# Two causal attention stages, the norm's root and TensorE filler products rearranged in an eight-stage kernel

## The reference

```python
x = x + jnp.tanh(g_xattn[0]) * _L0_xattn_ref(_layernorm(x), ctx_512, ...)   # causal, 16 heads, 64 keys used
x = x + jnp.tanh(g_ffn[0]) * _L0_ffn_ref(_layernorm(x), ...)                # top 8 of 64 experts' biases
x = x + jnp.tanh(g_xattn[1]) * _L1_xattn_ref(_layernorm(x), ctx_512, ...)   # latent, 1500 keys
x = x + jnp.tanh(g_ffn[1]) * _L1_ffn_ref(_layernorm(x), ...)                # ternary weights: mean |w| is needed
x = x + jnp.tanh(g_xattn[2]) * _L2_xattn_ref(_layernorm(x), ctx_512, ...)   # latent, queries with rope
x = x + jnp.tanh(g_ffn[2]) * _L2_ffn_ref(_layernorm(x), ...)                # Hadamard
x = x + jnp.tanh(g_xattn[3]) * _L3_xattn_ref(_layernorm(x), ctx_512, ...)   # causal again
x = x + jnp.tanh(g_ffn[3]) * _L3_ffn_ref(_layernorm(x), ...)                # 8 experts, one per row, and a shared one
return x

def causal(q, latent_kv):                     # layers 0 and 3, in short
    k, v = jnp.split(latent_kv @ Wkv_expand.T, 2, axis=-1)
    scores = jnp.einsum('bhqd,bhkd->bhqk', heads(q @ Wq.T), heads(k)) * inv_sqrt_d
    attn = jax.nn.softmax(jnp.where(causal, scores, min), axis=-1)
    return merge(jnp.einsum('bhqk,bhkd->bhqd', attn, heads(v))) @ Wout.T
```

## Time and profile before

| | us |
|---|---|
| median of 3 runs | 1805.56 (1804.91 to 1805.61) |
| profiled execution | 1805.35 |
| its span, first to last instruction | 1803.5 |
| busy in the span: PE, DVE, ACT, POOL | 1607.6, 922.1, 634.8, 670.5 |

### The profile page before, as it was taken

One profiled execution on the slowest core, in us unless ns is written; L12 is line 12 of the kernel. 1 busy time (PEld: TensorE's weight loads), 2 busy tenths in 40 slices (PEclk: granted clock), 3 DMA queues, 4 the chain that ended last, 5 costly groups with the idle time before them and its releaser, 6 DMA issues. The chain is left out here.

```text
span 1803.5 us, 38433 instructions
## 1 busy us (share of the span) xinstructions
PE 1607.6 (89%) x16648; PEld 1197.8 (66%) x16660; DVE 922.1 (51%) x1587; ACT 634.8 (35%) x941; POOL 670.5 (37%) x479
## 2 busy tenths in 40 slices
PE   6757889999999996668997999999999989777998
PEld 3335478888888875455443888888888745434466
DVE  2964165565665626772445565665655232147312
ACT  3323334454444431224011454544444221133221
POOL 2504255654446100640764645655441030232101
PEclk9977899999999997777998999999999989778999
DMA  7053365445554023001314555445540200512401
GB/s 122 1 164 95 85 140 131 101 110 113 118 124 93 26 79 105 0 1 67 94 23 102 131 126 117 98 106 118 113 92 16 82 0 0 194 56 63 134 24 59
DMA packets 64424, 154.39 MB, mean 86 GB/s; under 512 B 14428, under 2 KB 43676, under 8 KB 63344
## 3 DMA queue, kind: packets, MB, share of 16 engines
q1 hardware_dynamic: 63488, 150.10, 33.8%
q0 software_dynamic: 768, 1.84, 0.3%
HBM read 87.51 MB, written 5.51 MB: 52 GB/s over the span
## 5 line engine op out<-in xcount | busy, mean ns | idle before, releaser
L1390 DVE TENSOR_REDUCE latent_psW<-latent_psW 128x1 f32<-128x500 f32 x654 | 418.4, 682 | 221.7 <-PE latent_psW L1288 221.3
L1368 ACT ACTIVATE latent_w<-latent_psS 125x896 f32<-125x896 f32 x384 | 351.8, 919 | 432.8 <-PE latent_psS L1306 429.1
L1316 PEld LDWEIGHTS latent_psO<-latent_val,latent_w 125*64 125x64 f32 x10752 | 323.6, 138 | 30.6 <-issue 17.1
L1316 PE MATMUL latent_psO<-latent_val,latent_w 125*64 125x65 f32 x10752 | 340.9, 223 | 0.0
L1305 PE MATMUL latent_psS<-latent_qA,latent_kA 128*125 128x448 f32 x768 | 290.1, 378 | 3.9 <-DVE latent_qB L1406 2.3
L1306 PE MATMUL latent_psS<-latent_qB,latent_kB 128*125 128x448 f32 x768 | 282.3, 368 | 0.0
L1288 PE MATMUL latent_psW<-latent_kA,latent_qA 128*128 128x500 f32 x654 | 214.6, 398 | 12.5 <-DMA latent_qA<-latent_qh 11.2
L1305 PEld LDWEIGHTS latent_psS<-latent_qA,latent_kA 128*125 128x125 f32 x768 | 143.2, 186 | 30.9 <-ACT latent_w L1368 4.6
L1306 PEld LDWEIGHTS latent_psS<-latent_qB,latent_kB 128*125 128x125 f32 x768 | 143.5, 187 | 19.7
L1288 PEld LDWEIGHTS latent_psW<-latent_kA,latent_qA 128*128 128x128 f32 x654 | 125.3, 192 | 29.8 <-POOL latent_kB L1262 12.7
L794 POOL TENSOR_TENSOR latent_rawT<-latent_rawT,latent_ropeT 128x1000 f32<-128x1000 f32 x48 | 110.5, 2328 | 33.4 <-DMA latent_rawT<-in_ctx_cols 21.0
(11 more groups left out here) (332 smaller groups left out, 2110.7 us busy)
## 6 DMA issues: line engine op xcount, KB each, us to landing
latent_qA<-latent_qh SPq DMA_DIRECT2D x128, 112.0 KB, 2.3
latent_rawT<-in_ctx_cols SPq DMA_DIRECT2D x32, 375.0 KB, 5.2
latent_rawT<-in_ctx_cols SPq DMA_DIRECT2D x64, 187.5 KB, 5.8
latent_raw<-in_ctx SPq DMA_DIRECT2D x32, 375.0 KB
latent_kA<-latent_high SPq DMA_DIRECT2D x32, 375.0 KB, 3.7
latent_kB<-latent_high SPq DMA_DIRECT2D x32, 375.0 KB, 5.6
latent_kA<-latent_rawT SPq DMA_DIRECT2D x32, 375.0 KB, 5.2
experts_wgu<-in_L_gu SPq DMA_DIRECT2D x8, 1024.0 KB, 16.2
```

The lines of the kernel that those rows point to most:

```text
L1316: last = pe.matmul(sums[r:r + 64, c, :], w[t % ROUND][:, c * 128 + r:c * 128 + r + 64], val[b % 2][:, t, :], start=(t == 0 and c == 0), st ...
L1368: act.activation(w[t % ROUND][:, :].rearrange("p (h n) -> p h n", h=2), psS[0:KP, t % 2, :, 0:GH], ACT.Exp).then_inc(exp_done, 1)
L1390: dve.tensor_reduce(bank[:, THIRD + j:THIRD + j + 1], bank[:, 0:THIRD], mybir.AxisListType.X, ALU.max).then_inc(max_ready, 1)
```

## The change

In the causal stages the sixteen value products before the loop are gone. `expand_values(p)` makes the values of one pair in step p of the loop, behind the scores of that pair, into both halves of `ps_y`, the bank that the projection also uses; it waits until DVE has added pair p-4 and ACT has copied the values before. ACT's `take_values(p)` copies them in two pieces. The norm's root is the first thing on ACT; in stage 3 the turning also comes before the key products. In stage 0 the magnitudes come in eight DMAs and eight reductions, one behind the normalising of each pair, each of which takes the sum of the one before as its first element. The 64-row operands become 128-row ones whose lower half is cleared.

The weights of causal stage 3 are loaded in the Hadamard stage, and keep their place when the arena is made anew. In the top-8 stage all eight turns come first (two groups of four, one ACT copy each), then the eight products. In both query stages ACT makes the root before or between the fold copies. In the Hadamard stage POOL waits for DVE's small scalings. `keep_busy` puts products of the identity with itself, which nobody reads, into places where PE waits: 8 in `begin`, 14 and 36 in the top-8 stage, 18 in each latent stage, 16 in the Hadamard stage, 10 in causal stage 3, 18 in the experts stage.

```diff
+
+
+def keep_busy(pe, g, to, count):
+
+    for _ in range(count):
+        pe.matmul(to, g.ident[:, :], g.ident[:, :], start=True, stop=True)
...
+        self.root(act)
+        self.scalar_tiles(act)
+
+    def root(self, act):
         g = self.g
         if self.moments:
             act.wait_ge(self.mv_ready, NT)
         act.activation(self.std[:, :], g.mv[:, :, 1], ACT.Sqrt, bias=g.eps[0:TP, 0:1]).then_inc(self.std_ready, 1)
+
+    def scalar_tiles(self, act):
...
     w = Weights(nc, g, f"xattn{layer}_w")
-    w.wkv = w.put([DC, 2 * C], (None, d[f"L{layer}_kv"]))
-
-    w.ctxT = w.put([DC, B, 2, SK], (None, d["ctx_first"].rearrange("d (b e k) -> d b e k", b=B, e=2)))
+    w.wkv = w.put([128, 2 * C], (lambda v: v[0:DC, :], d[f"L{layer}_kv"]))
+
+    w.ctxT = w.put([128, B, 2, SK], (lambda v: v[0:DC, :, :, :], d["ctx_first"].rearrange("d (b e k) -> d b e k", b=B, e=2)))
+    w.pads = [w.wkv[DC:128, :], w.ctxT[DC:128, :, :, :]]
...
+                def turn_rows():
+                    norm.tensor(pe)
+                    pe.wait_ge(norm.xnT_ready, NT)
+
+                if layer:
+                    keep_busy(pe, g, ps_a[:, 0, 0:128], 10)
+                    turn_rows()
...
-                for b in range(B):
-                    pe.wait_ge(taken, n - 1)
-                    pe.matmul(ps_a[:, n % 2, 0:C], ctxT[:, b, :, :], wkv[:, C:2 * C],
-                              start=True, stop=True).then_inc(prod, 1)
-                    n += 1
-                norm.tensor(pe)
-                pe.wait_ge(norm.xnT_ready, NT)
+                if not layer:
+                    turn_rows()
...
+
+                def expand_values(p):
+                    wait_from(pe, x_done, p - 3)
+                    wait_from(pe, v_taken, p)
+                    for e in range(2):
+                        last = pe.matmul(ps_y[:, e * C:(e + 1) * C], ctxT[:, 2 * p + e, :, :], wkv[:, C:2 * C], start=True, stop=True)
+                    last.then_inc(v_done, 1)
...
                 def project(p):
                     pe.wait_ge(o_taken, p + 1)
+                    pe.wait_ge(v_taken, min(p + 4, NP))
                     if p >= 1:
...
                 for p in range(NP + 3):
                     if p < NP:
                         scores(p)
+                        expand_values(p)
+                    if 2 <= p < NP + 2:
+                        turn_weights(p - 2)
                     if 2 <= p < NP + 2:
                         output(p - 2)
...
             def _(act):
-                n = 0
-                for c in range(CC):
-                    for h in range(2):
+                def take_keys():
+                    for n in range(KV):
+                        c, h = n // 2, n % 2
                         act.wait_ge(prod, n + 1)
                         act.copy(kT[:, c, 8 * h:8 * h + 8, :],
                                  ps_a[:, n % 2, :].rearrange("p (b k) -> p b k", k=SK)).then_inc(taken, 1)
-                        n += 1
-                act.wait_ge(zeroed, 1)
-                for b in range(B):
+
+                norm.root(act)
+                if not layer:
+                    take_keys()
+                norm.scalar_tiles(act)
+                if layer:
+                    take_keys()
+                for n in range(KV, KV + QQ):
+                    m, h = (n - KV) // 2, n % 2
                     act.wait_ge(prod, n + 1)
-                    v = ps_a[:, n % 2, 0:C].rearrange("p (j e k) -> p j e k", j=HP, e=2)
-                    act.copy(values[0:64, b, :, 0, :], v[0:64, :, 0, :])
-                    act.copy(values[64:128, b, :, 1, :], v[64:128, :, 1, :]).then_inc(taken, 1)
-                    n += 1
-                norm.scalar(act)
-                for m in range(CC):
-                    for h in range(2):
-                        act.wait_ge(prod, n + 1)
-                        act.mul(qT[:, m, h * HALF:(h + 1) * HALF], ps_a[:, n % 2, 0:HALF], HD ** -0.5).then_inc(taken, 1)
-                        n += 1
+                    act.mul(qT[:, m, h * HALF:(h + 1) * HALF], ps_a[:, n % 2, 0:HALF], HD ** -0.5).then_inc(taken, 1)
+
+                def take_values(p):
+                    act.wait_ge(v_done, p + 1)
+                    if p == 0:
+                        act.wait_ge(zeroed, 1)
+                    v = ps_y[:, :].rearrange("p (b j e k) -> p b j e k", b=2, j=HP, e=2)
+                    for e in range(2):
+                        last = act.copy(values[64 * e:64 * e + 64, 2 * p:2 * p + 2, :, e, :], v[64 * e:64 * e + 64, :, :, e, :])
+                    last.then_inc(v_taken, 1)
 
                 def exp(p):
                     act.wait_ge(shifted, p + 1)
                     act.activation(sc[:, p % 3, :, :], sc[:, p % 3, :, :], ACT.Exp).then_inc(exp_done, 1)
 
-                def take(p):
+                def take_weights(p):
                     for h in range(2):
                         act.wait_ge(turned, 2 * p + h + 1)
                         if p >= 2 and h == 0:
                             act.wait_ge(o_done, p - 1)
                         act.copy(wT[:, p % 2, 4 * h:4 * h + 4, :],
                                  ps_t[:, h, :].rearrange("p (j n) -> p j n", j=4)).then_inc(wT_ready, 1)
+
+                def take_output(p):
                     act.wait_ge(o_done, p + 1)
                     act.copy(oT[:, :, p * TP:(p + 1) * TP].rearrange("q c (e s) -> q c e s", e=2),
                              ps_o[:, 0:256].rearrange("q (c e s) -> q c e s", c=2, e=2)[:, :, :, 0:S]).then_inc(o_taken, 1)
 
                 for p in range(NP + 2):
+                    if p < NP:
+                        take_values(p)
                     if p >= 2:
-                        take(p - 2)
+                        take_weights(p - 2)
+                        take_output(p - 2)
...
                 if magnitudes is not None:
-                    dve.wait_ge(lanes_came, 16)
-                    dve.tensor_reduce(magnitudes, lanes[:, :], X, ALU.add, apply_absolute_value=True).then_inc(lanes_summed, 1)
+                    dve.memset(lanes[:, 0, 0:1], 0.0).then_inc(lanes_summed, 1)
+
+                def sum_magnitudes(m):
+                    dve.wait_ge(lanes_came[m], 16)
+                    dve.wait_ge(lanes_summed, m + 1)
+                    dve.tensor_reduce(lanes[:, m + 1, 0:1] if m + 1 < CHUNKS else magnitudes, lanes[:, m, :], X, ALU.add,
+                                      apply_absolute_value=True).then_inc(lanes_summed, 1)
 
                 def soft(p):
                     u = p % 2
                         soft(p)
                     if 1 <= p <= NP:
                         normalise(p - 1)
+                        if magnitudes is not None:
+                            sum_magnitudes(p - 1)
 
 
 def top8_weights(nc, g, d):
     w = Weights(nc, g, "ffn0_w")
     w.rw = w.put([128, CC, 64], (None, d["L0_rw"].rearrange("(c p) n -> p c n", p=128)))
     w.bias = w.put([TP, 64], (None, d["L0_rb"].partition_broadcast(TP)))
-    w.eb = w.put([64, C], (None, d["L0_eb"]))
+    w.eb = w.put([128, C], (lambda v: v[0:64, :], d["L0_eb"]))
+    w.pads = [w.eb[64:128, :]]
     return w
 
 
...
                 ahead.clear(pool)
+                ahead.cleared_all(pool)
+                weights.pad(pool)
+                pool.memset(wT[E:128, :, :], 0.0).then_inc(wT_padded, 1)
...
                 for t in range(NT):
-                    if t >= 2:
-                        pe.wait_ge(wT_ready, t - 1)
-                    pe.transpose(ps_t[0:E, t % 2, 0:TP], e[:, t, :], g.ident[0:TP, 0:TP]).then_inc(turned, 1)
-                    pe.wait_ge(wT_ready, t + 1)
+                    pe.transpose(ps_t[0:E, t // 4, t % 4 * TP:(t % 4 + 1) * TP], e[:, t, :], g.ident[0:TP, 0:TP]).then_inc(turned, 1)
+                weights.padded_all(pe)
+                pe.wait_ge(wT_padded, 1)
+                for t in range(NT):
+                    pe.wait_ge(wT_ready, t // 4 + 1)
                     if t >= 2:
                         pe.wait_ge(y_taken, t - 1)
-                    pe.matmul(ps_y[0:TP, t % 2, 0:C], wT[:, t, :], eb[:, :], start=True, stop=True).then_inc(y_done, 1)
+                    pe.matmul(ps_y[0:TP, t % 2, 0:C], wT[:, t // 4, t % 4 * TP:(t % 4 + 1) * TP], eb[:, :], start=True, stop=True).then_inc(y_done, 1)
 
...
-                for t in range(NT):
-                    act.wait_ge(turned, t + 1)
-                    act.copy(wT[:, t, :], ps_t[0:E, t % 2, 0:TP]).then_inc(wT_ready, 1)
+                for half in range(2):
+                    act.wait_ge(turned, 4 * half + 4)
+                    act.copy(wT[0:E, half, :], ps_t[0:E, half, 0:4 * TP]).then_inc(wT_ready, 1)
...
+                    if n == 2:
+                        norm.root(act)
+                norm.scalar_tiles(act)
...
+                norm.root(act)
                 for h in range(NH):
...
+                keep_busy(pe, g, psO[:, 0:128], 18)
...
             def _(pool):
+                pool.wait_ge(had_ready, CC + 2)
...
```

(12 more changed lines are left out.)

66 lines of the change are left out of this document (49 added, 17 removed).

## The result

| | before | changed |
|---|---|---|
| median, us | 1805.39 (1804.91 to 1805.61, 4 runs) | 1749.14 (1744.18 to 1749.90, 4 runs) |
| profiled execution | 1805.35 | 1744.18 |
| its span | 1803.5 | 1742.4 |

What follows compares the result with a forecast made beforehand. The prediction saw barrier-separated stages, each bound by its own last chain, with gains where PE is slow or idle. Stage savings summed to 54.3 us, taking 1805.35 to 1751 us, range 1733 to 1771.

Steps and rivals of the forecast that it cites:

- 25.2 forecast for the front: Causal stage 3, barrier to first score product: 21.8 us instead of 47.0, so 25.2 us saved.
- 4.4 lost in the loop: Causal stage 3 loop: value products lengthen pairs from 5.76 to 6.9 us; four pairs counted, 4.4 us lost.
- rival (e): Causal stage 3: the early weight load does not do what it says; no loss, the turning covers it; no chance given.
- the clock term: Causal stage 3 front: fillers at the slow clock, then keys half fast, half slow, taken as 5.4 us.
- 9.1 forecast: Causal stage 0, net saving: 23.7 us saved at the front, 14.6 lost to magnitude pieces in the loop.
- rival (c): Causal loops: value products waiting for the residual add four pairs back close a ring; 12 + 5 us worse, 1768; chance 0.10.
- 5.8 forecast for the new order: Top-8 stage: turns grouped ahead of the products, bound by DVE's passes, save 5.8 us; its 36 fillers taken as 0.
- 10.6 and 1.9 forecast: Query stages 1 and 2: the earlier root removes waits before turning, saving 10.6 and 1.9 us.
- 4.0 forecast: Hadamard stage: POOL waits for DVE's scalings, PE starts earlier behind 16 fillers; 4.0 us saved, bounds 6 and -1.7.
- (a): Whole kernel: the clock does not come up, all fillers slow; 32 us worse, 1783, about 1767 if half; chance 0.12.
- (b): Whole kernel: the clock stays up through the turning; keys, queries, router products and folds fast; 17 us better, 1734; chance 0.15.
- (d): Causal loops: PE and DVE stop overlapping through the shared bank; 55 + 45 us worse, 1851; chance 0.03.

Runs made afterwards that it cites:

- e10: The kernel before the change, with only ACT's root moved ahead of its key and value copies in both causal stages; 1803.57 us, ratio 0.9985.
- e4: The changed kernel with the sixteen value products ahead of the causal loops again; 1756.07 us, ratio 0.9712.
- e2: The changed kernel with key, value and top-8 products over the 64 used rows again, fillers kept; 1755.69 us, ratio 0.9739.
- e1: The changed kernel with every filler product taken out; 1747.62 us, ratio 0.9682.
- second chip run: The changed kernel, unaltered, run again on another chip; median 1751.04 us, ratio 0.9679.
- e9_late_load: The changed kernel with causal stage 3's weights loaded in that stage again and POOL clearing the pads there; 1747.65 us, ratio 0.9689.

## Why the prediction was right, point by point

**The causal stage 3** was sized well: 25.2 forecast for the front, 26.0 measured; 4.4 lost in the loop, 3.2 measured (56.8 against 53.6). Its parts: the root alone 3.5 us (e10), the value products in the loop instead of ahead 7.4 us (e4), the cleared rows 4.5 us (e2), the ten fillers 0.5 us at most (e1). If the parts add, that leaves some 7 us of the 22.8 for the turning ahead of the keys, in the time in which PE waited for weights; this was not run alone. The early load is worth nothing in the total, as rival (e) had it; ahead of the turning it also keeps POOL's clearing away from DVE's scaling, which the prediction did not count.

**The cause of the clock term was wrong.** The step of the sum that failed is "the ten fillers take 2.1 us (fast) to 4.5 us (slow) ... Keys 3.6 us fast, 7.2 slow; I take 5.4", which let the fillers bring the clock up. The keys took 5.9 us with and without fillers, and 7.19 with 64-row operands. The clock comes up by the end of the keys when they are 128-row products, and it did not when they were 64-row ones; I had taken that edit for free. The fillers were not at the slow clock either, as I had them: they took 2.47 us. The Trainium skill (TensorE: Matmul & The Clock Gate, Part 4) says that turning does not count as work for the clock as other products do. By that rule fillers ahead of the turning are wasted. The two keys' rows agree with it; the router products of the top-8 stage, fast behind fillers and a turning in eight profiles of eleven and never without fillers, do not. The same page of the Trainium skill says in its closing table that a product over 32 rows takes as long as one over 128. For 64 rows the duration agrees at the same clock (1.13 us for four records in both kernels), and it can't be used for the granted clock, which differed.

**Causal stage 0.** 9.1 forecast, 7.7 and 2.7 measured. The first maximum came where it was forecast within 2.3 us, pairs at 7.65 for 7.8. The term that was too small is the loop's: 67.9 us from first maximum to last add, against 50.3 before, so 17.6 lost where I had 14.6. Of the 3 us between, 2.3 lie in the pairs of 8.5 and 9.0 us (10.96 on the second chip run): e9_late_load, which has no such pairs, has a loop of 65.6. In the pair of 8.5 us DVE's normalisation took 2.08 us instead of 1.23, beside a POOL product that began with it (54.24 and 54.29); e4_values_ahead, which has no value products in the loop, has that pair too (8.51). Behind it PE stood 4.86 us for the residual add and was then at half clock. This is rival (c) once, not in every pair; in e9_late_load the normalisation took 1.23 us, PE waited 2.43, the clock stayed up and the pairs were 7.64. The 2 us between the two profiles in the front have a like cause. In the first, DVE's scaling took 4.13 us and was over when POOL's key products began at 19.19; in the second the keys were faster (3.92 us instead of 5.53), POOL began at 17.54, beside the scaling, and that took 7.08 us; the turning was then full of waits, and the queries began 0.4 us later and at half clock (7.88 us instead of 6.28). All six profiles with keys of 3.9 us in stage 0 have a scaling of 7.1 us and queries of 7.8 to 9.1, so faster keys did not make this front shorter. In my account of stage 0 before, only 2.9 us of the reduction showed; e10 showed that with an early root it still ended at 57.0, its operands having landed at 39.8: the transfer and the reduction behind it alone made a front of that length.

**Top-8 stage.** 5.8 forecast for the new order; without fillers the stage was 5.5 us shorter than before. With fillers it was another 1.5 to 4.1 us shorter, which I had counted at 0 for the 36. Most of it is not theirs: the router products, behind the 14, took 3.27 us instead of 6.10 where the stage gained 4.1, and 6.10 as before where it gained 1.5. The sum has no term for them.

**Query stages.** 10.6 and 1.9 forecast; 12.2 to 13.0 and 4.0 to 4.1 measured, and undoing the root's place alone cost 11.9 and 4.1 us. The mechanism was the one named; in stage 2 the sum counted the wait only, and the clock behind it was missing: turning and the 32 records behind it took 4.0 and 4.46 us, where they took 4.6 and 5.91 in the kernel before.

**Hadamard stage.** 4.0 forecast, 2.7 measured. POOL's wait is worth 2.2 us, the fillers 0.4. I had PE start at 4.2 us after the barrier; the sixteen fillers ran until 5.3, at half clock for 3.4 us of it.

**Latent and experts stages.** The fillers made the first products of the latent stages faster (0.92 us for three records instead of 1.59), but DVE sets the pace there. Latent stage 2 came out 1.5 to 1.6 us longer, where I had 0.3 saved; e1_no_fillers puts that down to the fillers. Latent stage 1 shows nothing either way. In the experts stage the router products took 6.01 us as before; the 1.9 us saved are near the 1.5 forecast.

**The rivals.** (a) is out in its form, the granted clock being 0.95 and 0.85 in the top-8 stage; (b) did not happen, since in stage 3 the queries took 6.3 us but the keys 5.9, and the router products of the experts stage were as slow as before; (c) closed in one pair only; (d) did not happen. That the total came out within 2 us is partly luck: terms that were too small (stage 3, top-8, query stages) made up for terms that were too large (stage 0, Hadamard, latent 2).

## What to carry to other kernels

Products that nobody reads brought nothing in the total: they helped in one stage, by up to some 4 us and not alike in every execution, and cost 1.5 us in another. Clearing the idle half of an operand, so that a product spans 128 rows, was worth more than all fillers together, at no cost on PE. Look where an edit lets POOL and DVE run side by side: the clearing that the late load moved, and the key products that came earlier because PE was faster, lengthened a scaling by 1.8 and 2.9 us. Ask of work moved into a loop which engine sets that loop's pace: the magnitude sums cost 10 us in DVE's loop and nothing in DVE's wait ahead of it, and the value products were hidden but for 0.4 us a pair (6.16 against 5.76) as soon as they stood between the turning and the product that waits for its copy.

## What the runs showed of the hardware

- The granted clock depends on the rows that a product spans: in the kernel before it was 0.50 through 14.9 us of uninterrupted 64-row products; the same keys over 128 rows, half of them zero, ran at the full clock at least in part (3.78 to 6.44 us in eleven profiles, against 7.19 in all three with 64 rows).
- DVE's scalings are held up beside POOL's tensor products: 0.62 us for two alone, 4.56 and 4.89 beside POOL instructions of 2.34 to 2.36 us; 2.68 for eight alone, 11.78 and 11.85 beside POOL. The Trainium skill (SBUF — State Buffer, Who interferes with whom) says that such an operation of DVE and POOL share a port that one of them holds for a whole instruction, and that reductions do not take part. The trace agrees in both: two scalings took about as long as two POOL instructions, and a magnitude piece took 2.27 us beside POOL's key products (56.29 in the changed kernel) and 2.27 us with POOL idle (93.53 there). A normalisation with two operands in SBUF (line 641) took 2.08 us beside POOL and 1.23 alone.
- One kernel gave executions from 1744.6 to 1753.8 us with the same instructions. The two profiles of the changed kernel differ by 9.6 us, 8.3 of it by the end of query stage 1 (5.0 in causal stage 0), and stretches at 0.50 lie at other places in them. A difference of 2 to 3 us in one such stage of one profile is therefore no result by itself, in causal stage 0 not even one of 5.
